# Attention maxima: which two of a unit's four PSUM banks share one maximum instruction

## Chip, core and metric

The kernel runs on one core of one Trainium2 chip. The metric is the device time of one execution in microseconds (us), the median of several runs. TensorE is called PE here, VectorE DVE, ScalarE ACT, GpSimd POOL, and SyncE, which issues most of the DMAs, SP.

## What is computed

One attention layer over 4096 tokens of 256 channels with 16 heads of 16, beside a mixture of experts, then a second layer with a convolution, a recurrence, an MLP and another mixture of experts. The change touches the first layer's attention alone:

```python
xd = (x @ W_down).reshape(b, t, h, s)
keys = jnp.einsum('bthk,hik->bthi', xd, tokeys) * scale
queries = jnp.einsum('bthk,hik->bthi', xd, toqueries) * scale
values = jnp.einsum('bthk,hik->bthi', xd, tovalues)
dot = jnp.einsum('bqhs,bkhs->bhqk', queries, keys)
attn = jax.nn.softmax(dot, axis=-1)
out = jnp.einsum('bhqk,bkhs->bqhs', attn, values).reshape(b, t, e)
return out @ W_unify + b_unify
```

The softmax subtracts each row's maximum. The kernel finds that maximum from a first computation of the scores and uses it in a second one.

## The kernel before

The whole program is a row of phases, of which `attention_phase` is by far the longest. It takes the 16 heads in 8 pairs and the 4096 queries in 8 chunks of 512; one pair and one chunk are a **round**, and there are 64 rounds. A round has `U` = 16 **units**. The two heads of a pair lie in rows 0 to 63 and 64 to 127 of the operands, so that matmuls of both can be in the array together.

In each unit run two streams of scores. The maximum stream is ahead of the other by `LEAD` = 24 units, and its first 24 units are done by the phase before this one, so that 1000 of this phase's 1024 units have it:

- The **maximum stream**: `max_part` (matmul L1120) computes for head h and key chunk j the scores of 128 queries by 512 keys into bank 2h + j of `SA`, a PSUM tile of four banks (`scores_q`). DVE reduces each bank to one maximum per query. These go to `MPART`, of which there are two buffers that take turns by round (`max_parts` and `attention_max_parts` in the profile).
- The **probability stream**: `score_tile` (matmul L1126) computes the transposed scores with the maximum already taken off, into one of three banks `ST` (`scores_t`), ACT takes the exponential (L1202, `probs`), and `pv_part` (L1136) multiplies by the values: eight matmuls per unit, four per key tile. The profile has two records for each of these, so that x8 there is one key tile and x16 are both.

All engines work in order. PE's order in a unit is: bank 0 of the maximum stream, a score tile, bank 1, a tile, bank 2, a tile, bank 3, a tile. Where the value matmuls stand is set by the parity of the unit's number (`u % 2`):

```python
BLOCKS = ({(0, 1): (0,), (1, 1): (1,)}, {(1, 0): (0, 1)})
```

A key is (head, key chunk), its value the key tiles whose four matmuls follow there. An even unit has one key tile behind bank 1 and one behind bank 3. An odd unit has both key tiles, eight matmuls, behind bank 2 and so ahead of bank 3.

PE may fill a bank when DVE has reduced it in the unit before: `max_part` waits for the count `sa_free`, and DVE waits for the count `sa_ready`, both four per unit and in the order of the banks. On DVE, `body` calls for each unit `reduce_first` (before: one instruction, L1235, over banks 0 and 1), then `reduce_rest` (before: L1242, twice, one for bank 2 and one for bank 3). Once per round, in the unit that begins a new one of the maximum stream (an even unit), `negative_max` (L1249) stands between the two calls; it reduces the parts of the whole round to the final negated maximum, which POOL splits and SP writes into the operands. Four times in 16 rounds, always at unit 12, `recip` (L1255) stands behind `reduce_rest`.

Of the kernel before, what the change touches and what calls it, by code (L numbers as in the profile page):

```python
# [10 lines left out]
ALU = mybir.AluOpType  # L11
ACT = mybir.ActivationFunctionType
AX = mybir.AxisListType
# [6 lines left out]
CH = 512  # L20
# [59 lines left out]
class Phase:  # L80
# [11 lines left out]
    def sb(self, name, shape, dt=F32):  # L92
        return self.stack.enter_context(self.nc.sbuf_tensor(f"{self.name}_{name}", shape, dt))
# [6 lines left out]
    def ps(self, name, shape=(P, CH), dt=F32):  # L100
        return self.stack.enter_context(self.nc.psum_tensor(f"{self.name}_{name}_sums", list(shape), dt))

    def sem(self, name):
        return self.stack.enter_context(self.nc.semaphore(f"{self.name}_{name}"))
# [824 lines left out]
def attention_phase(nc, q_scratch, k_scratch, v_scratch, max_scratch, den_scratch, recip_scratch, att_scratch, DISP, lead, outs,  # L929
# [10 lines left out]
    with Phase(nc, "attention") as ph:  # L940
# [6 lines left out]
        MPART = [sb("max_parts0", [P, 2, 4, 8]), lead.MPART]  # L947
# [6 lines left out]
        SA = ps("scores_q", [P, 4 * CH])  # L954
# [9 lines left out]
        sa_ready, sa_free = sem("scores_q_ready"), sem("scores_q_reduced")  # L964
# [20 lines left out]
        def halves(body):  # L985
            for i in range(NP // 2):
                body(i, i == NP // 2 - 1)
# [236 lines left out]
        @block.vector  # L1224
        def _(dve):
            nc.vector.memset(PR[:, 12:16, :], 1.0).then_inc(filled, 1)
            dve.sem_inc(sa_free, 4 * LEAD + 4)
            dve.sem_inc(neg_ready, 1)
            dve.sem_inc(pv_done, 3)
            dve.sem_inc(recip_out, 32)  # L1230

            def reduce_first(par, u, s):
                first = 2 * (u % 4)
                dve.wait_ge(sa_ready, 4 * s + 2)
                nc.vector.tensor_reduce(MPART[par][:, 0, u // 4, first:first + 2], SA[:, 0:2 * CH].rearrange("p (j k) -> p j k", j=2),  # L1235
                                        AX.X, ALU.max).then_inc(sa_free, 2)

            def reduce_rest(par, u, s):
                first = 2 * (u % 4)
                for j in range(2):  # L1240
                    dve.wait_ge(sa_ready, 4 * s + j + 3)
                    nc.vector.tensor_reduce(MPART[par][:, 1, u // 4, first + j:first + j + 1], SA[:, (2 + j) * CH:(3 + j) * CH],  # L1242
                                            AX.X, ALU.max).then_inc(sa_free, 1)

            def negative_max(par, s, splits):

                dve.wait_ge(sa_free, 4 * s + 8)
                dve.wait_ge(msplit, 2 * splits)
                nc.vector.tensor_reduce(NEG[:, :, :], MPART[par][:, :, :, :], AX.X, ALU.max, negate=True)\  # L1249
                    .then_inc(neg_ready, 1)  # L1250

            def recip(n):
                dve.wait_ge(den_in, 32 * (n + 1))
                dve.wait_ge(recip_out, 32 * (n + 1))
                nc.vector.reciprocal(RD[:, :], DEN[:, :]).then_inc(recip_done, 1)  # L1255

            def body(i, last):
                for r in range(HALF):
                    g = i * HALF + r
                    for u in range(U):  # L1260
                        s, s_round, s_unit = g * U + u + LEAD, r + (u + LEAD) // U, (u + LEAD) % U
                        has_max = not (last and s_round >= HALF)
                        if has_max:
                            reduce_first(s_round % 2, s_unit, s)
                        if s_unit == 0 and not (last and s_round > HALF):
                            negative_max((s_round - 1) % 2, s - 1, g + (u + LEAD) // U - 1)
                        if has_max:
                            reduce_rest(s_round % 2, s_unit, s)
                        if r % 4 == 1 and u == RECIP_AT:
                            recip(4 * i + r // 4)  # L1270

            halves(body)
# [1196 lines left out]
```

## Time and profile before

| | us |
|---|---|
| median of 3 runs | 3727.38 |
| lowest, highest | 3726.7, 3727.47 |
| profiled execution, its own time | 3727.63 |
| its span, first to last instruction | 3725.8 |
| PE busy | 3608.3 |
| DVE busy | 3209.2 |
| ACT busy | 2643.1 |
| mean granted clock of PE, share of full speed | 0.985 |

The page gives for each engine its busy time and, for each group of instructions, the idle time of the engine just before them with what ended it. Views of the trace give the same for a stretch, or the instructions one by one with their start. PEld is the loading of weights on PE, which may lie under a running matmul. The starts of matmuls are modelled from their records; an instruction's duration is longer than the distance to the next start where both overlap in the pipeline.

### The profile page before, as it was taken

How to read it: one execution, taken by the hardware profiler on the slowest of the kernel's cores; microseconds unless marked ns; L12 is line 12 of the kernel's file. 1: busy time of each engine (PE TensorE's matmuls, PEld its weight loads, DVE VectorE, ACT ScalarE, POOL GpSimd, SP SyncE). 2: the span in 40 equal slices, each digit the busy share in tenths (PEclk: the TensorE clock that was granted, in tenths of full speed). 3: DMA queues.
4: the chain of work that ended last, by engine and by line, in shares of the span. 5: the costliest groups of instructions: out<-in, count | busy, mean ns of one | idle time of the engine just before them, and what ended most of it. 6: DMA issues, size and time to landing. Idle time of an engine off the chain costs nothing. (4 is left out here: it accounts for less than half of the span.)

```text
span 3725.8 us, 78041 instructions
## 1 busy us (share of the span) xinstructions
PE 3608.3 (97%) x31366; PEld 2064.9 (55%) x31366; DVE 3209.2 (86%) x4509; ACT 2643.1 (71%) x4951; POOL 369.9 (10%) x331
## 2 busy tenths in 40 slices
PE   8799899999999999999999999999998989999998
PEld 6487444444444444444444444444445668888887
DVE  6667799999999999999999999999975757766664
ACT  3455598989888989888999888999896442223332
POOL 0123200000000000000000000000002203403323
PEclk9899899999999999999999999999999999999999
DMA  4910322021122113112202202200012000122332
GB/s 139 249 38 18 113 23 30 4 30 26 7 23 22 17 10 34 18 9 24 29 4 30 26 7 24 32 6 7 4 32 82 34 2 29 55 93 66 82 85 39
DMA packets 299888, 149.50 MB, mean 40 GB/s; under 512 B 218527, under 2 KB 278057, under 8 KB 296980
## 3 DMA queue, kind: packets, MB, share of 16 engines
q1 hardware_dynamic: 287252, 133.97, 19.4%
q0 software_dynamic: 12288, 10.70, 1.7%
q8 instruction: 240, 3.93, 0.5%
q14 instruction: 108, 0.88, 0.1%
HBM read 86.46 MB, written 64.18 MB: 40 GB/s over the span
## 5 line engine op out<-in xcount | busy, mean ns | idle before, releaser
L1202 ACT ACTIVATE probs<-attention_scores_t_sums 128x512 f32<-128x512 f32 x4096 | 2142.2, 597 | 246.0 <-PE attention_scores_t_sums L1126 243.8
L1126 PE MATMUL attention_scores_t_sums<-q_operand,k_operand 50*128 50x512 f32 x2048 | 702.9, 443 | 15.4 <-ACTq L1216 13.8
L1120 PE MATMUL attention_scores_q_sums<-attention_k_operand,attention_q_operand 48*128 48x512 f32 x2048 | 699.8, 439 | 0.0
L1126 PE MATMUL attention_scores_t_sums<-attention_q_operand,attention_k_operand 50*128 50x512 f32 x2048 | 698.6, 443 | 0.0
L1120 PE MATMUL attention_scores_q_sums<-k_operand,q_operand 48*128 48x512 f32 x1952 | 669.6, 440 | 0.0
L1242 DVE TENSOR_REDUCE max_parts<-attention_scores_q_sums 128x1 f32<-128x512 f32 x1008 | 639.1, 670 | 1.6 <-PE attention_scores_q_sums L1120 1.6
L1242 DVE TENSOR_REDUCE attention_max_parts<-attention_scores_q_sums 128x1 f32<-128x512 f32 x992 | 628.9, 670 | 0.0
L1235 DVE TENSOR_REDUCE max_parts<-attention_scores_q_sums 128x2 f32<-128x1024 f32 x504 | 605.7, 1202 | 8.6 <-PE attention_scores_q_sums L1120 8.5
L1136 PE MATMUL attention_o_psum_sums<-probs,attention_v_heads 128*32 128x256 f32 x8208 | 602.8, 388 | 0.0
L1136 PE MATMUL attention_o_psum_sums<-probs,v_heads 128*32 128x256 f32 x8192 | 602.1, 388 | 0.0
L1235 DVE TENSOR_REDUCE attention_max_parts<-attention_scores_q_sums 128x2 f32<-128x1024 f32 x496 | 596.8, 1203 | 0.0
L1120 PEld LDWEIGHTS attention_scores_q_sums<-attention_k_operand,attention_q_operand 48*128 48x128 f32 x2048 | 319.9, 184 | 388.8 <-issue 119.2
L1120 PEld LDWEIGHTS attention_scores_q_sums<-k_operand,q_operand 48*128 48x128 f32 x1952 | 306.3, 185 | 371.7 <-issue 115.7
L1126 PEld LDWEIGHTS attention_scores_t_sums<-q_operand,k_operand 50*128 50x128 f32 x2048 | 337.3, 185 | 17.3 <-ACTq L1216 14.0
L1126 PEld LDWEIGHTS attention_scores_t_sums<-attention_q_operand,attention_k_operand 50*128 50x128 f32 x2048 | 335.2, 184 | 19.7 <-ACT probs L1202 17.6
L1136 PEld LDWEIGHTS attention_o_psum_sums<-probs,v_heads 128*32 128x32 f32 x8192 | 187.6, 108 | 276.8 <-issue 148.7
L1136 PEld LDWEIGHTS attention_o_psum_sums<-probs,attention_v_heads 128*32 128x32 f32 x8208 | 188.1, 108 | 275.1 <-issue 147.7
L1096 POOL TENSOR_TENSOR attention_neg_max_split<-attention_neg_max,attention_zero 128x8 fp32r<-128x8 f32 x63 | 12.7, 202 | 2318.7 <-DVE attention_neg_max L1249 2318.7
L1975 ACT ACTIVATE mlp_silu<-mlp_gate_sums,mlp_b_gate 128x512 f32<-128x512 f32 x64 | 44.2, 691 | 200.1 <-PE mlp_gate_sums L119 200.1
L119 PE MATMUL experts_out_sums<-experts_w_low,experts_hidden_high 128*128 128x256 f32 x512 | 144.9, 283 | 0.0
L119 PE MATMUL experts_out_sums<-experts_w_high,experts_hidden_high 128*128 128x256 f32 x512 | 143.7, 281 | 0.0
L119 PE MATMUL experts_out_sums<-experts_w_high,experts_hidden_low 128*128 128x256 f32 x512 | 143.7, 281 | 0.0
(330 smaller groups left out, 4687.7 us busy)
## 6 DMA issues: line engine op xcount, KB each, us to landing
expert_rows<-attention_empty_rows SPq DMA_DIRECT2D x16, 516.0 KB, 5.6
v_scratch<-value_chunk SPq DMA_DIRECT2D x16, 512.0 KB, 5.4
w_whole<-in_L_ffn_ew SPq DMA_DIRECT2D x8, 1024.0 KB, 7.3
experts_w_whole<-in_L_ffn_ew SPq DMA_DIRECT2D x8, 1024.0 KB, 5.7
q_operand<-q_scratch SPq DMA_DIRECT2D x24, 256.0 KB, 4.7
k_operand<-k_scratch SPq DMA_DIRECT2D x24, 256.0 KB, 6.4
attention_q_operand<-q_scratch SPq DMA_DIRECT2D x24, 256.0 KB, 4.8
attention_k_operand<-k_scratch SPq DMA_DIRECT2D x24, 256.0 KB, 6.5
```

The costliest lines, as they stand in the source:

```text
L119: mm = nc.tensor.matmul(out, lhs[l], rhs[r], start=first and n == 0, stop=last and n == 2)
L1096: nc.gpsimd.tensor_tensor(MS[par][:, :, 0, :], NEG[:, :, :], ZERO[:, :, :], ALU.add).then_inc(msplit, 1)
L1120: nc.tensor.matmul(SA[:, (2 * h + j) * CH:(2 * h + j + 1) * CH], QOP[b][64 * h:64 * h + ROWS, qt * P:(qt + 1) * P], KOP[b][64 * h:64 * h + ...
L1126: nc.tensor.matmul(ST[bank_n][:, :], KOP[b][64 * h:64 * h + ROWS + 2, kt * P:(kt + 1) * P], QOP[b][64 * h:64 * h + ROWS + 2, c * CH:(c + 1 ...
L1136: mm = nc.tensor.matmul(OP[64 * h + 32 * side:64 * h + 32 * side + 32, :], VH[b][:, 2 * u + j, h, :], PR[:, u % 4 * 4 + 2 * (1 - h) + j, s ...
L1202: nc.scalar.activation(PR[:, tile, :], ST[bank_n][:, :], ACT.Exp).then_inc(st_free, 1)
L1235: nc.vector.tensor_reduce(MPART[par][:, 0, u // 4, first:first + 2], SA[:, 0:2 * CH].rearrange("p (j k) -> p j k", j=2), AX.X, ALU.max).th ...
L1242: nc.vector.tensor_reduce(MPART[par][:, 1, u // 4, first + j:first + j + 1], SA[:, (2 + j) * CH:(3 + j) * CH], AX.X, ALU.max).then_inc(sa_ ...
L1975: nc.scalar.activation(G[m % 2], GP[m % 2][:, :], ACT.Silu, bias=BG[:, m:m + 1])\
```

## The change

`reduce_first` now reduces bank 0 alone. `reduce_rest` reduces bank 1 alone, and then banks 2 and 3 with one instruction, which waits until both are full and releases both at once. The new helper `reduce_single` holds the instruction for banks 0 and 1. The four maxima of a unit go to the same places of `MPART` as before. The number of instructions, their shapes and the counts of the semaphores per unit stay as they are.

```diff
--- before.py
+++ after.py
@@ -1229,18 +1229,22 @@
             dve.sem_inc(pv_done, 3)
             dve.sem_inc(recip_out, 32)
 
+            def reduce_single(par, u, s, j):
+                part = 2 * (u % 4) + j
+                dve.wait_ge(sa_ready, 4 * s + j + 1)
+                nc.vector.tensor_reduce(MPART[par][:, 0, u // 4, part:part + 1], SA[:, j * CH:(j + 1) * CH],
+                                        AX.X, ALU.max).then_inc(sa_free, 1)
+
             def reduce_first(par, u, s):
+                reduce_single(par, u, s, 0)
+
+            def reduce_rest(par, u, s):
+                reduce_single(par, u, s, 1)
                 first = 2 * (u % 4)
-                dve.wait_ge(sa_ready, 4 * s + 2)
-                nc.vector.tensor_reduce(MPART[par][:, 0, u // 4, first:first + 2], SA[:, 0:2 * CH].rearrange("p (j k) -> p j k", j=2),
+                dve.wait_ge(sa_ready, 4 * s + 4)
+                nc.vector.tensor_reduce(MPART[par][:, 1, u // 4, first:first + 2],
+                                        SA[:, 2 * CH:4 * CH].rearrange("p (j k) -> p j k", j=2),
                                         AX.X, ALU.max).then_inc(sa_free, 2)
-
-            def reduce_rest(par, u, s):
-                first = 2 * (u % 4)
-                for j in range(2):
-                    dve.wait_ge(sa_ready, 4 * s + j + 3)
-                    nc.vector.tensor_reduce(MPART[par][:, 1, u // 4, first + j:first + j + 1], SA[:, (2 + j) * CH:(3 + j) * CH],
-                                            AX.X, ALU.max).then_inc(sa_free, 1)
 
             def negative_max(par, s, splits):
```

On DVE, the stretch of the attention in which a new round of the maximum stream begins (`attention_neg_max` is the final maximum, `max_parts` and `attention_max_parts` the two buffers of parts). Before:

```order
L1242 TENSOR_REDUCE attention_max_parts<-attention_scores_q_sums 128x1 [waits attention_scores_q_ready] x2
L1235 TENSOR_REDUCE max_parts<-attention_scores_q_sums 128x2 [waits attention_scores_q_ready]
L1249 TENSOR_REDUCE attention_neg_max<-attention_max_parts 128x8 [waits attention_neg_max_split_done,attention_scores_q_reduced]
L1242 TENSOR_REDUCE max_parts<-attention_scores_q_sums 128x1 [waits attention_scores_q_ready] x2
L1235 TENSOR_REDUCE max_parts<-attention_scores_q_sums 128x2 [waits attention_scores_q_ready]
```

After, at the same place:

```order
L1235 TENSOR_REDUCE attention_max_parts<-attention_scores_q_sums 128x1 [waits attention_scores_q_ready] x2
L1245 TENSOR_REDUCE attention_max_parts<-attention_scores_q_sums 128x2 [waits attention_scores_q_ready]
L1235 TENSOR_REDUCE max_parts<-attention_scores_q_sums 128x1 [waits attention_scores_q_ready]
L1253 TENSOR_REDUCE attention_neg_max<-attention_max_parts 128x8 [waits attention_neg_max_split_done,attention_scores_q_reduced]
L1235 TENSOR_REDUCE max_parts<-attention_scores_q_sums 128x1 [waits attention_scores_q_ready]
L1245 TENSOR_REDUCE max_parts<-attention_scores_q_sums 128x2 [waits attention_scores_q_ready]
```

The two-bank maximum has moved from the head of a unit to its end, and the final maximum now stands between the two single-bank ones.

On PE nothing moves. This is one odd unit, the same before and after: banks 0, 1 and 2 of `scores_q`, each with a tile of the other stream (`scores_t`), then the eight value matmuls, then bank 3 and its tile:

```order
L1120 MATMUL attention_scores_q_sums<-k_operand0,q_operand0 128x512 [waits attention_scores_q_reduced]
L1126 MATMUL attention_scores_t1_sums<-q_operand0,k_operand0 128x512 [waits attention_scores_t_used]
L1120 MATMUL attention_scores_q_sums<-k_operand0,q_operand0 128x512 [waits attention_scores_q_reduced]
L1126 MATMUL attention_scores_t2_sums<-q_operand0,k_operand0 128x512 [waits attention_scores_t_used]
L1120 MATMUL attention_scores_q_sums<-k_operand0,q_operand0 128x512 [waits attention_scores_q_reduced]
L1126 MATMUL attention_scores_t0_sums<-q_operand0,k_operand0 128x512 [waits attention_scores_t_used]
L1136 MATMUL attention_o_psum_sums<-probs,v_heads0 32x256 [waits attention_scores_t_used]
L1136 MATMUL attention_o_psum_sums<-probs,v_heads0 32x256 x7
L1120 MATMUL attention_scores_q_sums<-k_operand0,q_operand0 128x512 [waits attention_scores_q_reduced]
L1126 MATMUL attention_scores_t1_sums<-q_operand0,k_operand0 128x512 [waits attention_scores_t_used]
```

Each L1120 still waits for its own bank's count; what has changed is which maximum raises it.

## Rows read from the trace of the kernel before

**Rows 1.** Page, part 1: busy us, share, count by engine.
```profile
PE 3608.3 (97%) x31366; PEld 2064.9 (55%) x31366; DVE 3209.2 (86%) x4509; ACT 2643.1 (71%) x4951; POOL 369.9 (10%) x331
```

**Rows 2.** Stretch 1000 to 2500 us: engines' busy time (count), PEclk, DMA, GB/s.
```profile
1000.00:2500.00 1500.00, 1498.71 (x15376) 667.25 (x15376) 1498.00 (x1973) 1348.55 (x2603) 16.19 (x80) 1.00 0.19 20
```

**Rows 3.** Waits, 500 to 2760 us: total us, times, longest.
```profile
DVE max_parts L1235 <- PE attention_scores_q_sums L1120: 2.0, 6, 0.4
```

**Rows 4.** Timeline of DVE from 1504 us: start us, duration us, instructions.
```profile
1504.44 1.21 DVE L1235 TENSOR_REDUCE attention_max_parts<-attention_scores_q_sums 128x2 f32<-128x1024 f32 x1
1505.57 1.27 DVE L1242 TENSOR_REDUCE attention_max_parts<-attention_scores_q_sums 128x1 f32<-128x512 f32 x2
1506.77 1.21 DVE L1235 TENSOR_REDUCE attention_max_parts<-attention_scores_q_sums 128x2 f32<-128x1024 f32 x1
...
1509.10 1.21 DVE L1235 TENSOR_REDUCE attention_max_parts<-attention_scores_q_sums 128x2 f32<-128x1024 f32 x1
```

**Rows 5.** L1249 (one buffer), L1255: ns min/median/max, first and last start.
```profile
L1249 DVE TENSOR_REDUCE attention_neg_max<-max_parts x32: 194/197/220, 447.9 to 2768.8; 128x8 f32<-128x64 f32 x32
...
L1255 DVE RECIPROCAL recip_den<-denominators x16: 329/330/336, 495.9 to 2742.9; 128x32 f32<-128x32 f32 x16
```

**Rows 6.** Timeline of PE, 1505.8 to 1510 us: one odd and one even unit.
```profile
1505.84 0.49 PE L1120 MATMUL attention_scores_q_sums<-attention_k_operand,attention_q_operand 48*128 48x512 f32 x1
...
1506.17 0.40 PE L1120 MATMUL attention_scores_q_sums<-attention_k_operand,attention_q_operand 48*128 48x512 f32 x1
...
1506.41 0.40 PE L1120 MATMUL attention_scores_q_sums<-attention_k_operand,attention_q_operand 48*128 48x512 f32 x1
1506.74 1.07 PE L1136 MATMUL attention_o_psum_sums<-probs,attention_v_heads 128*32 128x256 f32 x16
1507.74 0.50 PE L1120 MATMUL attention_scores_q_sums<-attention_k_operand,attention_q_operand 48*128 48x512 f32 x1
...
1508.08 0.45 PE L1120 MATMUL attention_scores_q_sums<-attention_k_operand,attention_q_operand 48*128 48x512 f32 x1
...
1508.36 0.39 PE L1120 MATMUL attention_scores_q_sums<-attention_k_operand,attention_q_operand 48*128 48x512 f32 x1
...
1509.26 0.50 PE L1120 MATMUL attention_scores_q_sums<-attention_k_operand,attention_q_operand 48*128 48x512 f32 x1
...
1509.60 0.39 PE L1120 MATMUL attention_scores_q_sums<-attention_k_operand,attention_q_operand 48*128 48x512 f32 x1
```

**Rows 7.** Timeline of PEld, the load after 1507.98 us.
```profile
1508.03 0.18 PEld L1120 LDWEIGHTS attention_scores_q_sums<-attention_k_operand,attention_q_operand 48*128 48x128 f32 x1
```

**Rows 8.** Timeline of DVE, attention's start; in brackets idle time before.
```profile
426.37 1.29 DVE L1242 TENSOR_REDUCE max_parts<-attention_scores_q_sums 128x1 f32<-128x512 f32 x2 [0.43 <-PE attention_scores_q_sums L1120]
429.03 1.22 DVE L1235 TENSOR_REDUCE max_parts<-attention_scores_q_sums 128x2 f32<-128x1024 f32 x1 [1.38 <-PE attention_scores_q_sums L1120]
```

**Rows 9.** Timeline of PE, attention's start, granted clock 0.5.
```profile
423.38 0.79 PE L1120 MATMUL attention_scores_q_sums<-k_operand,q_operand 48*128 48x512 f32 x1
...
425.54 0.79 PE L1120 MATMUL attention_scores_q_sums<-k_operand,q_operand 48*128 48x512 f32 x1
...
428.29 0.62 PE L1120 MATMUL attention_scores_q_sums<-k_operand,q_operand 48*128 48x512 f32 x1
...
431.73 0.59 PE L1120 MATMUL attention_scores_q_sums<-k_operand,q_operand 48*128 48x512 f32 x1
```

**Rows 10.** L1235 into one of two buffers: count, durations, starts.
```profile
L1235 DVE TENSOR_REDUCE max_parts<-attention_scores_q_sums x504: 1148/1202/1225, 424.7 to 2766.3; 128x2 f32<-128x1024 f32 x168
```

**Rows 11.** Stretches behind the attention: busy one, one with a wait.
```profile
2893.00:2950.00 57.00, 53.89 (x271) 37.86 (x273) 56.65 (x11) 26.49 (x41) 16.93 (x4) 1.00 0.00 1
3046.00:3054.00 8.00, 5.88 (x21) 5.14 (x22) 6.89 (x6) 2.94 (x3) 0.00 (x0) 0.57 0.01 2
```

**Rows 12.** PE's waits, 2893 to 2950 us, then 3030 to 3060 us.
```profile
PE router_logit_parts_sums L1626 <- ACT router_hidden L1676: 3.1, 4, 0.8
...
PE mlp_squares_sums L1920 <- DVEq L2011: 3.9, 1, 3.9
```

## Prediction, made before the changed kernel ran

> **What bounds the kernel now.** I read the busy shares first: PE is busy for 97% of the span, DVE for 86%, ACT for 71% [rows 1]. These are means over stages that differ. In the attention, between 1000 and 2500 us, DVE is busy for 1498.00 of 1500 us, PE for 1498.71 and ACT for 1348.55, at a granted clock of 1.00 [rows 2]. PE and DVE both look full, so busy time alone doesn't name the bound. The waits do: from 500 to 2760 us DVE waits for PE for 2.0 us in all, in six places [rows 3]. DVE has its next maximum ready whenever it is done with the last one; it is the bound.
>
> The timeline of DVE shows its beat [rows 4]. A two-bank maximum (L1235) starts at 1504.44, 1506.77 and 1509.10 us, every 2.33 us, which is one unit. From its start to that of the first single-bank maximum (L1242) pass 1.13 us (1504.44 to 1505.57), and the two singles take the other 1.20 (1505.57 to 1506.77). An instruction's own time is a little longer, 1.21 us for two banks and 1.27 for two singles together, since its end lies under the start of the next. Two units, an odd and an even one, take 4.66 us. Over the whole stage, the final maxima of one buffer, one in every second round of 16 units, run 32 times from 447.9 to 2768.8 us [rows 5]; a round takes 2320.9 / 62 = 37.43 us, which is 8 pairs of units at 4.65 and 0.2 for the final maximum itself.
>
> Then PE's timeline of one pair [rows 6]. I call the four banks 0 to 3: 0 and 1 are the first head's, 2 and 3 the second's. In the odd unit L1120 fills bank 0 at 1505.84, bank 1 at 1506.17 and bank 2 at 1506.41; then come eight matmuls of probabilities with values (L1136, in the row as x16) at 1506.74, and only at 1507.74 is bank 3 filled. In the even unit banks 0 and 1 follow at 1508.08 and 1508.36, then four value matmuls, then banks 2 and 3 at 1509.26 and 1509.60. So **banks 0 and 1 are filled close together in both kinds of unit** (0.33 and 0.28 us apart), banks 2 and 3 in the even unit only (0.34 us); in the odd one they are 1507.74 - 1506.41 = 1.33 us apart. This decides the case, since a two-bank maximum needs both its banks full before it begins and gives both back only when it ends.
>
> **The change, part by part.**
>
> *Work of DVE.* Per unit one maximum over two banks and two over one bank, before and after, of the same shapes. Taken alone this is worth nothing: 1.13 + 1.20 = 2.33 us in either order.
>
> *The window of the pair.* Between the end of a two-bank maximum and the start of the next, both its banks must be filled again, if DVE isn't to stop. DVE gives 2.33 - 1.21 = **1.12 us** for that [rows 4]. Before, banks 0 and 1 need: 0.05 us from the end of the maximum (1506.77 + 1.21 = 1507.98) to PE's next weight load for L1120 (1508.03) [rows 4, 7]; 0.10 for loading weights into an idle array (a first matmul takes 0.49, a following one 0.39 [rows 6]); 0.33 or less to the second bank; 0.39 for its matmul; 0.12 until DVE starts (matmul at 428.29 for 0.62, so done at 428.91; L1235 at 429.03 [rows 8, 9]). Together at most 0.05 + 0.10 + 0.33 + 0.39 + 0.12 = 0.99 us. It fits in 1.12, which is why DVE hardly ever waits.
>
> After, banks 2 and 3 have to pass through the same window. In the **odd unit** the chain is: release 0.05; weights 0.10, and 0.33 from the matmul of bank 2 to the value matmuls (1506.41 to 1506.74); 1.00 from there to the matmul of bank 3 (1506.74 to 1507.74); 0.50 for that one [rows 6]; 0.12 to the start of the maximum. Sum 0.05 + 0.43 + 1.00 + 0.50 + 0.12 = 2.10 us. The window has 1.12, so **DVE stops for 0.98 us in every odd unit**. Nothing hides it: DVE works in order, and the next unit's bank 0 stands behind the waiting instruction, though it is full by then. PE can't make it up either; it can't fill bank 2 before the last maximum has read it.
>
> In the **even unit** the need is 0.05 + 0.10 + 0.24 + 0.39 + 0.12 = 0.90 us (0.24 being the closest spacing, 1506.17 to 1506.41 [rows 6]). It fits, with 0.22 to spare. PE is at bank 2 of the even unit in time: from bank 3 of the odd one it takes 1509.26 - 1507.74 = 1.52 us, and the maximum over the odd unit's banks ends 0.50 + 0.12 + 1.21 = 1.83 us after the same point.
>
> *Single maxima on banks 0 and 1.* Each bank has 2.33 - 0.67 = 1.66 us between its own maxima (a single takes 1.27 less the 0.60 by which the second starts later, 0.67 [rows 4]), and needs 0.05 + 0.50 + 0.12 = 0.67. That DVE may now begin after bank 0 alone, and that both banks come free earlier, gains nothing, as DVE isn't waiting there today [rows 3].
>
> *What moves with it.* The final maximum (L1249) now stands behind one single-bank maximum, not behind the pair; its 0.2 us per round stay in DVE's stream between an odd and an even unit and cost what they cost before, and POOL, which waits for it, has it a little sooner in the unit. The reciprocal (L1255, 0.33 us, 16 times [rows 5]) stands behind an even unit; its time will now lie in the stop of the odd unit that follows, a gain of 16 x 0.33 = 5 us. ACT has about 10% to spare [rows 2] and gets more.
>
> *The sum.* The code has one two-bank maximum per unit in 1024 - 24 = 1000 units, 504 of them in the one buffer [rows 10]; half of them are odd. 500 x 0.98 = 490, less 5, is **+485 us**. The profiled execution took 3727.63 us (span 3725.8), the median is 3727.38; so 3727.6 + 485 = about **4213 us**, 13.0% slower.
>
> *Bounds.* Three terms are not seen in just this position. The value matmuls after a lone matmul of bank 2 may start 0.24 instead of 0.33 us after it; DVE's start may take 0.04 (matmul at 425.54 for 0.79, done at 426.33; L1242 at 426.37 [rows 8, 9]) instead of 0.12: together 0.17 less, +400 us. The release may take 0.19 instead of 0.05 (1504.44 + 1.21 = 1505.65 to the matmul at 1505.84 [rows 4, 6], though PE was just leaving its value matmuls there): 0.14 more, +555 us. I take the middle values since they come from the same kind of instruction and wait: 0.12 is from a two-bank maximum, 0.05 from a release that PE stood ready for.
>
> **The rivals.**
>
> *No stop, 3722 to 3728 us.* DVE's work is the same, and the change only turns its pattern round against PE's. For it: DVE's floor of 4.66 us a pair is untouched, and the even unit fits in its window. It would decide if the matmul of bank 3 could come before the value matmuls in the odd unit. Against it: the order on PE is fixed in the code, and 2.10 us don't go into 1.12. This is also the case in which the kernel isn't slower. It ends within 0.2% of today's time, as only the 2.0 us of waits and the 5 us of reciprocals could go.
>
> *A smaller stop, 3970 to 4120 us.* If weights or matmul starts overlap the value block more than they do now, 0.2 to 0.5 us of the 0.98 vanish, each 0.1 us being worth 50 us. Nothing in the rows shows such an overlap: the x16 block is followed by L1120 after 1.00 us [rows 6].
>
> *The clock falls, over 4290 us.* PE will now idle twice in a pair, by about 0.3 us each: once before bank 2 of the even unit (1.83 + 0.05 against 1.52) and once before bank 2 of the odd one. At the lower clock level, 1.2 GHz, a pair took 431.73 - 423.38 = 8.35 us [rows 9], against 4.66 + 0.98 = 5.64. If a tenth of the pairs ran so, 50 x 2.7 = 135 us more, 4348 us; if half, 675 more. What speaks against it: from 2893 to 2950 us PE was busy for 53.89 of 57 us, with waits of up to 0.8 us, and the granted clock stayed at 1.00 [rows 11, 12]. It fell to 0.57 in the stretch from 3046 to 3054 us, where PE had waited 3.9 us at one piece [rows 11, 12]. The Trainium skill, TensorE: Matmul & The Clock Gate, section "A second HAM failure mode: psum-queue depth-cycling", says that a kernel which cycles through PSUM banks can idle so often in short pieces that the clock oscillates between its two levels. By that rule this change would pay twice, for the stop and for the clock; the stretch with 0.8 us waits at 1.00 disagrees with it for waits as short as these.
>
> *Even units stop too.* If their 0.22 us to spare are gone, each 0.1 us over costs 50 us. This lies in the upper part of the range.
>
> **How the numbers follow.** The stop in odd units (even units included if they add a little), 4120 to 4290: 0.87. Smaller stop: 0.04. Clock: 0.05. No stop: 0.04. The range 4110 to 4290 us takes in both bounds. A measurement of this kernel can tell about 0.2%, 7 us, from no change. Slower by more than that: 0.95; within it: 0.04; faster: 0.01, as nothing shortens DVE's stream by over 7 us.
>
> **What the profile after would show.** DVE's busy time stays near 3209 us, and its idle time before the two-bank maximum (now L1245), released by L1120, becomes about 490 us, in about 500 waits of nearly 1 us, none in even units. The two-bank maxima start alternately 2.33 and 3.31 us apart. The final maxima come every 8 x 5.64 + 0.2 = 45.3 us. The granted clock stays at 1.00. ACT's idle time before L1202 grows by nearly the whole 485 us. I am wrong if DVE waits in both kinds of unit (then PE is slower than its rows say), if the stop in the odd unit is far from 0.98, or if the clock leaves 1.00 during the attention.

## The result and the profile after

| | before | changed |
|---|---|---|
| median, us | 3727.43 (3726.7 to 3730.67, 4 runs) | 4213.09 (4210.83 to 4215.01, 4 runs) |
| profiled execution, us (span) | 3727.63 (3725.8) | 4215.01 (4213.2) |
| ratio, 95% interval | | 1.130, 1.1282 to 1.1318 |

The changed kernel is 485.7 us slower (4213.09 - 3727.43); 485 were forecast. These rows are from the page of the changed kernel: first busy time, share of the span and count by engine (compare [rows 1]), then groups of instructions: busy us, mean ns | idle time of the engine just before them and what ended it.

```profile
PE 3737.7 (89%) x31366; PEld 2027.9 (48%) x31366; DVE 3253.1 (77%) x4509; ACT 2701.5 (64%) x4951; POOL 369.3 (9%) x331
...
L1202 ACT ACTIVATE probs<-attention_scores_t_sums 128x512 f32<-128x512 f32 x4096 | 2200.7, 596 | 674.2 <-PE attention_scores_t_sums L1126 669.0
...
L1245 DVE TENSOR_REDUCE max_parts<-attention_scores_q_sums 128x2 f32<-128x1024 f32 x504 | 614.1, 1219 | 225.1 <-PE attention_scores_q_sums L1120 225.1
L1245 DVE TENSOR_REDUCE attention_max_parts<-attention_scores_q_sums 128x2 f32<-128x1024 f32 x496 | 604.2, 1218 | 222.4 <-PE attention_scores_q_sums L1120 222.4
...
L1235 DVE TENSOR_REDUCE max_parts<-attention_scores_q_sums 128x1 f32<-128x512 f32 x1008 | 645.1, 678 | 5.1 <-PE attention_scores_q_sums L1120 5.1
```

Nearly all the new idle time of DVE stands before the two-bank maximum, L1245: 225.1 + 222.4 = 447.5 us over the whole program. In the kernel before, the page has 8.6 us before its two-bank maximum, 2.0 of them between 500 and 2760 us [rows 3]. Before the single maxima there are 5.1 us. DVE's timeline shows where in the pair of units (compare [rows 4]):

```profile
1505.11 1.21 DVE L1245 TENSOR_REDUCE max_parts<-attention_scores_q_sums 128x2 f32<-128x1024 f32 x1
1506.24 1.28 DVE L1235 TENSOR_REDUCE max_parts<-attention_scores_q_sums 128x1 f32<-128x512 f32 x2
1508.40 1.22 DVE L1245 TENSOR_REDUCE max_parts<-attention_scores_q_sums 128x2 f32<-128x1024 f32 x1 [0.89 <-PE attention_scores_q_sums L1120]
1509.54 1.28 DVE L1235 TENSOR_REDUCE max_parts<-attention_scores_q_sums 128x1 f32<-128x512 f32 x2
1510.74 1.21 DVE L1245 TENSOR_REDUCE max_parts<-attention_scores_q_sums 128x2 f32<-128x1024 f32 x1
```

In the rows, DVE alternates between two-bank maxima (x1) and two single ones (x2), with one stop of 0.89 us. The two-bank maxima start 3.29 and 2.34 us apart in turn; a pair of units takes 1510.74 - 1505.11 = 5.63 us, before 4.66. PE's side of the stop, in the timelines of its matmuls and of its weight loads (compare [rows 6, 7]; the brackets give the idle time before and what ended it):

```profile
1504.05 0.49 PE L1120 MATMUL attention_scores_q_sums<-attention_k_operand,attention_q_operand 48*128 48x512 f32 x1 [0.34 <-DVE max_parts L1245]
...
1506.38 0.49 PE L1120 MATMUL attention_scores_q_sums<-attention_k_operand,attention_q_operand 48*128 48x512 f32 x1 [0.36 <-DVE max_parts L1245]
...
1506.80 1.07 PE L1136 MATMUL attention_o_psum_sums<-probs,v_heads 128*32 128x256 f32 x16
1507.80 0.50 PE L1120 MATMUL attention_scores_q_sums<-attention_k_operand,attention_q_operand 48*128 48x512 f32 x1
...
1506.37 0.18 PEld L1120 LDWEIGHTS attention_scores_q_sums<-attention_k_operand,attention_q_operand 48*128 48x128 f32 x1 [0.79 <-DVE max_parts L1245]
```

The first row is bank 2 of the even unit, the second that of the odd one. From there it is the chain of the prediction, link by link: the even unit's pair ends at 1505.11 + 1.21 = 1506.32; bank 2's weights load 0.05 us later; the value matmuls begin 0.43 us after that; bank 3 follows 1.00 us after them and takes 0.50, to 1508.30; DVE starts at 1508.40.

### The profile page after: what moved, and what is told of

Read it like the earlier page. It is cut to its first block and busy times, and to the rows that moved or that the text cites. A ratio compares the mean times of both kernels' runs of the same rounds, so it can differ in the third digit from the quotient of the medians.

```text
span 4213.2 us, 78041 instructions
## 1 busy us (share of the span) xinstructions
PE 3737.7 (89%) x31366; PEld 2027.9 (48%) x31366; DVE 3253.1 (77%) x4509; ACT 2701.5 (64%) x4951; POOL 369.3 (9%) x331
## 5 line engine op out<-in xcount | busy, mean ns | idle before, releaser
L1202 ACT ACTIVATE probs<-attention_scores_t_sums 128x512 f32<-128x512 f32 x4096 | 2200.7, 596 | 674.2 <-PE attention_scores_t_sums L1126 669.0
L1120 PE MATMUL attention_scores_q_sums<-attention_k_operand,attention_q_operand 48*128 48x512 f32 x2048 | 749.2, 444 | 183.9 <-DVE max_parts L1245 92.1
L1120 PE MATMUL attention_scores_q_sums<-k_operand,q_operand 48*128 48x512 f32 x1952 | 716.7, 446 | 172.9 <-DVE attention_max_parts L1245 86.4
L1245 DVE TENSOR_REDUCE max_parts<-attention_scores_q_sums 128x2 f32<-128x1024 f32 x504 | 614.1, 1219 | 225.1 <-PE attention_scores_q_sums L1120 225.1
L1245 DVE TENSOR_REDUCE attention_max_parts<-attention_scores_q_sums 128x2 f32<-128x1024 f32 x496 | 604.2, 1218 | 222.4 <-PE attention_scores_q_sums L1120 222.4
L1126 PE MATMUL attention_scores_t_sums<-q_operand,k_operand 50*128 50x512 f32 x2048 | 749.4, 446 | 15.6 <-ACTq L1216 13.8
L1126 PE MATMUL attention_scores_t_sums<-attention_q_operand,attention_k_operand 50*128 50x512 f32 x2048 | 743.5, 446 | 0.0
L1235 DVE TENSOR_REDUCE max_parts<-attention_scores_q_sums 128x1 f32<-128x512 f32 x1008 | 645.1, 678 | 5.1 <-PE attention_scores_q_sums L1120 5.1
L1235 DVE TENSOR_REDUCE attention_max_parts<-attention_scores_q_sums 128x1 f32<-128x512 f32 x992 | 635.8, 679 | 0.0
L1120 PEld LDWEIGHTS attention_scores_q_sums<-attention_k_operand,attention_q_operand 48*128 48x128 f32 x2048 | 322.4, 185 | 630.8 <-DVE max_parts L1245 209.3
L1120 PEld LDWEIGHTS attention_scores_q_sums<-k_operand,q_operand 48*128 48x128 f32 x1952 | 308.1, 185 | 598.8 <-DVE max_parts L1245 197.5
L1126 PEld LDWEIGHTS attention_scores_t_sums<-q_operand,k_operand 50*128 50x128 f32 x2048 | 321.3, 185 | 27.5 <-ACTq L1216 14.0
L1126 PEld LDWEIGHTS attention_scores_t_sums<-attention_q_operand,attention_k_operand 50*128 50x128 f32 x2048 | 320.1, 185 | 29.5 <-ACT probs L1202 17.5
```

The lines of the kernel that those rows point to most:

```text
L1120: nc.tensor.matmul(SA[:, (2 * h + j) * CH:(2 * h + j + 1) * CH], QOP[b][64 * h:64 * h + ROWS, qt * P:(qt + 1) * P], KOP[b][64 * h:64 * h + ...
L1126: nc.tensor.matmul(ST[bank_n][:, :], KOP[b][64 * h:64 * h + ROWS + 2, kt * P:(kt + 1) * P], QOP[b][64 * h:64 * h + ROWS + 2, c * CH:(c + 1 ...
L1202: nc.scalar.activation(PR[:, tile, :], ST[bank_n][:, :], ACT.Exp).then_inc(st_free, 1)
L1235: nc.vector.tensor_reduce(MPART[par][:, 0, u // 4, part:part + 1], SA[:, j * CH:(j + 1) * CH], AX.X, ALU.max).then_inc(sa_free, 1)
L1245: nc.vector.tensor_reduce(MPART[par][:, 1, u // 4, first:first + 2], SA[:, 2 * CH:4 * CH].rearrange("p (j k) -> p j k", j=2), AX.X, ALU.ma ...
```

## Experiments

All kernels were timed beside the kernel before, and their ratios are to it. What a **pair** of units took is worked out from the final maxima, which run every 16 units: (last start - first start) / 62 rounds, less 0.2 us, by 8; in b3 and b4, where DVE has time to spare for the final maximum, nothing is taken off. The 0.2 is the duration of the final maximum; by starts it costs DVE 0.12 to 0.13 us, which makes a pair 0.01 us longer throughout and changes no comparison.

| kernel | median, us | ratio, 95% interval | pair, us | expected, us |
|---|---|---|---|---|
| a1, new pair in even units only | 3915.40 | 1.0508 (1.0490 to 1.0525) | 5.03 | 3912 |
| a2, new pair in odd units only | 3914.05 | 1.0503 (1.0485 to 1.0520) | 5.03 | 3902 |
| b1, four singles | 3791.91 | 1.0176 (1.0159 to 1.0193) | 4.78 | 3797 |
| a3, singles, bank 2 late begun | 3945.29 | 1.0584 (1.0566 to 1.0601) | 5.09 | 3942 |
| a4, singles, bank 2 late released | 3981.43 | 1.0682 (1.0665 to 1.0700) | 5.16 | 3942 |
| b2, singles, both | 4245.23 | 1.1394 (1.1375 to 1.1413) | 5.69 | 4242 |
| b3, changed, value matmuls split | 3859.09 | 1.0357 (1.0339 to 1.0374) | 4.93 | 3862 |
| b4, before, value matmuls split | 3860.20 | 1.0356 (1.0339 to 1.0374) | 4.93 | 3862 |
| c1, changed, half of the block | 3997.35 | 1.0729 (1.0711 to 1.0747) | 5.20 | 3985 |
| c2, before, block behind bank 0 | 4339.66 | 1.1622 (1.1589 to 1.1655) | 5.80 | 4210 to 4270 |
| c3, changed, block behind bank 0 | 4122.04 | 1.1059 (1.1040 to 1.1077) | 5.39 | 4050 |

### Which unit pays (a1, a2)

The edit, shortened (the words in brackets stand for code):

```diff
 def reduce_first(par, u, s):
-    reduce_single(par, u, s, 0)
+    if u % 2 == 0: (bank 0 alone)            # a2: u % 2 == 1
+    else: (banks 0 and 1 together)
 def reduce_rest(par, u, s):
+    if u % 2 == 0: (bank 1, then banks 2 and 3 together)
+    else: (bank 2, bank 3)
```

> The changed pairing (banks 2 and 3 share a maximum) in even units only; odd units keep the pair over banks 0 and 1. Theory of the window: bank 2 comes free late, at the end of the even unit's pair, and in the odd unit that follows the eight value matmuls stand between banks 2 and 3. From the start of the even pair: 1.21 + 0.05 + 0.43 + 1.00 + 0.50 + 0.04 = 3.23 us until bank 3 of the odd unit can be reduced; DVE's own work until then is 1.13 + 1.13 + 0.60 = 2.86. A stop of 0.37 us in 500 pairs of units: +185 us, 3912 us. Rival 1 (only the late start counts, a pair waits for its second bank): the even unit fills banks 2 and 3 close together, so no cost, 3727 us. Rival 2 (a pair at the end of a unit costs by itself, whatever the unit): half of the 485 us, 3970 us.

> The changed pairing in odd units only. Theory of the window: bank 2 is released by the even unit's single maximum. From its start 0.67 + 0.05 + 0.43 + 1.00 + 0.50 + 0.10 = 2.75 us until both banks of the odd unit are full; DVE's own four singles take 2.40. A stop of 0.35 us in 500 pairs: +175 us, 3902 us. So the two halves of the change together cost less (360) than the whole (485). Rival 1 (only the late start counts): the whole cost, 4213 us. Rival 2 (each pair at the end of a unit costs the same): 3970 us.

Both rivals fall: neither kernel is at 3727 or 4213, nor at 3970. Each half costs 186 to 188 us, the whole 485: they don't add up. An estimate from the rows of the kernel before says why. There, from the start of the even unit's maximum over bank 2 to a full bank 3 in the odd unit, the chain over PE takes 0.67 + 0.05 + 0.43 + 1.00 + 0.50 + 0.04 = 2.69 us. DVE's own work in between is 0.60 + 0.60 + 1.13 + 0.60 = 2.93 us, so 0.24 are to spare. Each half moves the balance by about 0.60, one single maximum: a1 lengthens the chain, a2 takes work away from beside it. That leaves a stop of 0.60 - 0.24 = 0.36 us in each half, and 1.20 - 0.24 = 0.96 in the whole.

In a1 it is a *single* maximum that waits, bank 3's of the odd unit:

```profile
1505.90 2.43 DVE L1243 TENSOR_REDUCE attention_max_parts<-attention_scores_q_sums 128x2 f32<-128x1024 f32 x2
1508.25 0.68 DVE L1235 TENSOR_REDUCE attention_max_parts<-attention_scores_q_sums 128x1 f32<-128x512 f32 x1
1509.13 1.89 DVE L1235 TENSOR_REDUCE attention_max_parts<-attention_scores_q_sums 128x1 f32<-128x512 f32 x3 [0.21 <-PE attention_scores_q_sums L1120]
```

There the even unit fills its two banks close together and begins in time; what costs is that it gives bank 2 back late.

### What in the pair pays: its instruction, its late start, its late release (b1, a3, a4, b2)

Each unit has four single maxima, of the form below: one starts when `ready` banks of the unit are full, and raises `sa_free` by `freed`. Banks 0 and 1 have (1, 1) and (2, 1) in all four kernels. With (ready, freed) for bank 2 and bank 3: b1 (3, 1) and (4, 1); a3 (4, 1) and (4, 1); a4 (3, 0) and (4, 2); b2 (4, 0) and (4, 2).

```diff
+def reduce_single(par, u, s, h, j, ready, freed):
+    part = 2 * (u % 4) + j
+    dve.wait_ge(sa_ready, 4 * s + ready)
+    ins = nc.vector.tensor_reduce(MPART[par][:, h, u // 4, part:part + 1], SA[:, (2 * h + j) * CH:(2 * h + j + 1) * CH],
+                                  AX.X, ALU.max)
+    if freed:
+        ins.then_inc(sa_free, freed)
```

> Four single maxima, each with its own wait and its own release; no pair anywhere. Theory of the window: no stop, DVE alone sets the time with 8 x 0.60 = 4.80 us per pair of units against 4.66: +70 us, 3797 us. This is the base for the kernels with a late start or a late release. Rival (PE's or ACT's own limit was behind the cost): well above 3797.

> No two-bank maximum at all: four single ones, each releasing its own bank; but that of bank 2 waits until bank 3 is full as well, as the pair does. Theory of the window: DVE's own work is 8 x 0.60 = 4.80 us per pair of units (+70 us against 4.66); bank 2's maximum of the odd unit can start 0.67 + 0.05 + 0.43 + 1.00 + 0.50 + 0.04 = 2.69 us after that of the even unit, and DVE's own four singles take 2.40: a stop of 0.29. 5.09 us per pair, +215, 3942 us. Rival (the form: a two-bank instruction over banks 2 and 3 is what is slow): 3797 us, singles only.

> Four single maxima, each starting as soon as its own bank is full; but bank 2 is released only together with bank 3, as the pair does. Theory of the window: bank 3's maximum of the odd unit can start 0.67 + 0.05 + 0.43 + 1.00 + 0.50 + 0.04 = 2.69 us after that of the even unit, which released bank 2, against 2.40 of DVE's own work: a stop of 0.29. 5.09 us per pair, 3942 us, as with the late start. Rival 1 (only the late start counts): 3797 us. Rival 2 (the form of the instruction): 3797 us.

> Four single maxima, but bank 2's waits for bank 3 to be full and doesn't release: the late start and the late release of the pair, without its instruction. Theory of the window: from the start of bank 3's maximum in the even unit 0.67 + 0.05 + 0.43 + 1.00 + 0.50 + 0.04 = 2.69 us to the start of bank 2's in the odd one, DVE's own work 1.80: a stop of 0.89. 5.69 us per pair, +515, 4242 us; more than the sum of the two alone. Rival (the form of the instruction): 3797 us. Rival (the two parts add up): 70 + 145 + 145 = 360, 4087 us.

The form of the instruction is out: b2 has no two-bank maximum and still costs what the changed kernel does. Against b1, the late start costs 153 us, the late release 190, both together 453, more than their sum of 343. This is the same spare time again: with a single in place of the two-bank maximum DVE's work beside the chain is 5 x 0.60 = 3.00 us, not 2.93, which leaves 3.00 - 2.69 = 0.31 us to spare, so that each part alone stops DVE for 0.29 and both for 0.89.

The late release came 39 us above its number. What it had in place of the expected start of DVE is in these rows, first of a3, then of a4; in each the matmul of bank 3 and the maximum that waited for it:

```profile
1502.35 0.49 PE L1120 MATMUL attention_scores_q_sums<-attention_k_operand,attention_q_operand 48*128 48x512 f32 x1
...
1502.88 4.88 DVE L1235 TENSOR_REDUCE max_parts<-attention_scores_q_sums 128x1 f32<-128x512 f32 x8 [0.22 <-PE attention_scores_q_sums L1120]
```

```profile
1506.89 0.49 PE L1120 MATMUL attention_scores_q_sums<-attention_k_operand,attention_q_operand 48*128 48x512 f32 x1
...
1507.49 0.69 DVE L1235 TENSOR_REDUCE max_parts<-attention_scores_q_sums 128x1 f32<-128x512 f32 x1 [0.29 <-PE attention_scores_q_sums L1120]
```

From the end of the matmul to the start are 0.04 us in a3 (1502.84 to 1502.88) and 0.11 in a4 (1507.38 to 1507.49), for the same shape. The maximum of a4 raises its count by 2, that of a3 by 1. In b2, the maximum that waits raises nothing, and it starts 0.04 after its matmul too (1504.85 + 0.50 = 1505.35 to 1505.39). The two-bank maximum of the changed kernel raises by 2 and has 0.10 (1508.30 to 1508.40). I had put 0.04 for a4; 500 x 0.07 = 35 us are most of the difference. One more thing differs between a3 and a4 at this place: the maximum ahead of the waiting one raises its count in a3 and not in a4. This was not tested alone.

### Where the value matmuls stand (b3, b4)

```diff
-BLOCKS = ({(0, 1): (0,), (1, 1): (1,)}, {(1, 0): (0, 1)})
+BLOCKS = ({(0, 1): (0,), (1, 1): (1,)}, {(0, 1): (0,), (1, 1): (1,)})
```

b3 has this on the changed kernel, b4 on the kernel before.

> The changed kernel, but the odd unit's value matmuls stand as the even unit's do, four behind bank 1 and four behind bank 3, so that nothing stands between banks 2 and 3. Theory of the window: banks 2 and 3 need 0.90 to 0.99 us in a window of 1.12, no stop of this kind; but PE now changes between scores and values four times per pair of units, not three, so PE sets the time: 2 x (0.24 x 2 + 0.33 x 2 + (0.57 + 0.10) x 2) = about 4.93 us. +135 us, 3862 us. Rival (the pairing over banks 2 and 3 costs wherever the value matmuls stand): 4213 us or more.

> The kernel before with the same placement of the value matmuls, four behind bank 1 and four behind bank 3 in both kinds of unit. Theory of the window: PE's four changes set the time here too, 4.93 us per pair of units, 3862 us: with this placement the two pairings cost the same, within 10 us. Rival (the pairing as such): 3727 to 3862, and the changed kernel with this placement some 485 us above it.

With nothing between banks 2 and 3, the new pairing costs nothing against the old: 3859.09 and 3860.20 us. Both are some 134 us slower than the kernel before, since PE changes four times per pair between the two kinds of matmul, not three, and now sets the time. (The terms of the expectation for b3 add up to 4.96 us, not to 4.93; the rows of b3 give 4 x (0.34 + 0.32 + 0.57) = 4.92.) As PE sets the time, a stop of DVE below 4.93 - 4.66 = 0.27 us per pair would not show in the total; the 0.98 of the changed kernel would. The trace settles the rest: from 500 to 2700 us, DVE waited before L1245 four times, for 1.8 us in all. Stretch 500 to 2700 us of b3: busy time of PE, PEld, DVE, ACT and POOL, then granted clock, DMA share, GB/s.

```profile
500.00:2700.00 2200.00, 2199.66 (x21398) 813.24 (x21398) 2159.82 (x2745) 1947.84 (x3623) 22.33 (x110) 1.00 0.18 19
```

PE is busy throughout there, and DVE has 2200 - 2160 = 40 us to spare.

### How long the block is (c1)

In the odd unit, only one of the two key tiles is multiplied, so four of the eight value matmuls are missing and the attention's sums lack that tile. (The flag that starts the sums was moved to the tile that is left; this part of the edit is not shown.)

```diff
-BLOCKS = ({(0, 1): (0,), (1, 1): (1,)}, {(1, 0): (0, 1)})
+BLOCKS = ({(0, 1): (0,), (1, 1): (1,)}, {(1, 0): (1,)})
```

> The changed kernel with half of the odd units' value matmuls left out (one key tile's four of the eight between banks 2 and 3; the sums lack that tile). Theory of the window: the chain gets 0.43 us shorter (0.57 from the value matmuls to bank 3, not 1.00): a stop of 0.55, 5.18 us per pair of units, +265 less 5, 3985 us. So 0.43 us less between the banks takes away 0.43 us per pair in full, 215 to 225 us. Rival (PE's total work sets the time): PE was never full in the changed kernel, and no change, 4213 us.

```profile
1501.91 1.28 DVE L1235 TENSOR_REDUCE max_parts<-attention_scores_q_sums 128x1 f32<-128x512 f32 x2
1503.65 1.22 DVE L1245 TENSOR_REDUCE max_parts<-attention_scores_q_sums 128x2 f32<-128x1024 f32 x1 [0.46 <-PE attention_scores_q_sums L1120]
```

The wait fell from 0.89 to 0.46 us, by exactly the 0.43 by which the block is shorter, and the time by 216 us = 500 x 0.43. The 3985 us expected were a slip in the sum: 500 x 0.55 less 5 is 270, and 3727 + 270 = 3997, which is what was measured.

### The same trap for the old pairing (c2, c3)

```diff
-BLOCKS = ({(0, 1): (0,), (1, 1): (1,)}, {(1, 0): (0, 1)})
+BLOCKS = ({(0, 1): (0,), (1, 1): (1,)}, {(0, 0): (0, 1)})
```

c2 has this on the kernel before, c3 on the changed one.

> The kernel before (pair over banks 0 and 1), but with the odd unit's eight value matmuls behind bank 0, so that they now stand between the banks of that pair. Theory of the window: 0.05 + 0.43 + 1.00 + 0.50 + 0.10 = 2.08 us in a window of 1.12, a stop of 0.96 or a little more, since PE comes to bank 0 of the odd unit straight from four value matmuls and may be 0.1 us late: 5.63 to 5.75 us per pair, 4210 to 4270 us. The old pairing then costs what the new one does. Rival (the pairing at the unit's end is what costs): 3727 us.

> The changed kernel with the same placement, the odd unit's eight value matmuls behind bank 0. The pair over banks 2 and 3 now has its banks close together in both kinds of unit; the value matmuls stand between banks 0 and 1, which have single maxima. Theory of the window: no stop before the pair beyond 0.05 us. But by PE's order four and eight value matmuls now stand close to each other around bank 0, and bank 1 of the odd unit comes late for its single maximum: a stop of about 0.6 there, 5.3 us per pair, 4050 us; below the old pairing with the same placement by 100 to 220 us. Rival (the pairing at the unit's end is what costs): 4213 us and more.

The direction is as expected: with the block behind bank 0, the old pairing is the slower one, by 218 us, and the two-bank maximum over banks 0 and 1 stops as the new one does in the changed kernel:

```profile
1502.46 1.22 DVE L1235 TENSOR_REDUCE attention_max_parts<-attention_scores_q_sums 128x2 f32<-128x1024 f32 x1 [1.03 <-PE attention_scores_q_sums L1120]
...
1508.55 1.23 DVE L1235 TENSOR_REDUCE attention_max_parts<-attention_scores_q_sums 128x2 f32<-128x1024 f32 x1 [1.34 <-PE attention_scores_q_sums L1120]
```

Both sizes were missed, c2 by 70 us beyond its upper end and c3 by 72. For c2 the trace accounts for nearly all of it:

- The usual pair takes 5.78 us, not at most 5.75 (at 2655.26 and 2661.04 us two such stops end). PE comes to bank 0 of the odd unit 0.15 us late from its value matmuls, not 0.1 (it was free at 1504.80 + 1.21 + 0.05 = 1506.06 and its matmul starts at 1506.21). That is about 15 us.
- One odd unit per round waits longer, here 1.34 for 1.03 us, together about 20 us. It is unit 1, where the value matmuls also wait for ACT's copy of the last round's sums (`o_copied`): PE waited for that copy 46 times between 500 and 2700 us, and never in the kernel before.
- The clock fell once in the attention, to 0.50 from 2669.8 to 2683.5 us. Two stops there were 3.53 and 3.27 us long, about 5 us more than usual in all.
- What follows the last final maximum, the last units without maxima among it, ran at a low clock for longer: 4341.1 - 3349.6 = 991 us to the end, where the kernel before has 957 and the changed one 955. That is 34 us. The row shows its first part; the last three figures are the granted clock, the share of the DMA engines and GB/s:

```profile
3345.00:3410.00 65.00, 62.10 (x359) 22.12 (x355) 3.71 (x6) 37.95 (x73) 9.79 (x6) 0.63 0.15 36
```

Three of c2's four executions, the profiled one among them, took 4337 to 4343 us at a mean clock of 0.976 to 0.978; the fourth took 4316.49 at 0.985. That it lacked the low stretch is likely, but it has no profile.

In c3 the end is longer too, 4121.9 - 3133.9 = 988 us, 31 more than before, at 0.50 from 3155 to 3180 us. Most of the rest is the pair, 5.39 us for 5.3: 0.62 are the stop before bank 1, as put, 0.06 a short delay of the two-bank maximum behind the even unit's singles (1504.56 to 1505.82 are 1.26, not 1.20), and unit 1 has its longer wait here as well (0.85 for 0.53).

## Why the prediction was right

**The bound.** That DVE was the engine to look at, and that only the start of the two-bank maximum counted, held: 447.5 us of its new idle time stand before L1245.

**The window.** The time that refilling banks 2 and 3 needs in the odd unit was put at 0.05 + 0.43 + 1.00 + 0.50 + 0.12 = 2.10 us; the rows of the changed kernel give 0.05 + 0.43 + 1.00 + 0.50 + 0.10 = 2.08. The stop by starts was put at 0.98 and is 0.97 (after 1506.24 two singles take 0.60 each, to 1507.44, and 1508.40 is 0.96 later; over the pair 5.63 - 4.66 = 0.97). c1 and b3 show that the block between the banks is the cause, and a3, a4 and b2 that it works by late start and late release together.

**The even unit.** It fits with its 0.22 us to spare: of 1000 two-bank maxima 504 waited, all 500 of the odd units and four of even ones (the first of the attention for 1.37 us, three others for 0.26 each). Two places in which PE idles were named; they are there, with 0.34 and 0.36 us.

**The middle values of the uncertain terms.** The release (0.05) and the distance from bank 2 to the value matmuls (0.33 beside 0.10 of weights) were right as taken, and so was the start of DVE, for a reason not known then: 0.11 belongs to an instruction that raises a count by 2, 0.04 to one that raises it by 1. The lower bound of that term didn't apply. That the reason is the raise by 2 rests on a3, a4 and b2, with the reservation made there.

**Final maxima** were to come every 45.3 us; they start from 452.7 to 3257.8 us, which is 45.2.

**How close, and how much of it is luck.** 485 forecast and 485.7 measured are closer than the terms are known: a term read to 0.01 us is worth 5 us over 500 units, and the four executions lie 4 us apart. Two terms were a little off, in opposite directions: the stop was 0.97 for 0.98 (5 us too much), and the 16 reciprocals gave back 3 us and not 5, since a stop behind one shows as 0.69 us in place of 0.89 (16 x 0.20). The mechanism and its size are no luck; the match to 1 us is.

**What was off.** The idle time before L1245 was to be about 490 us and is 447.5: the view counts from the end of the instruction before, which lies 0.08 us behind the next possible start, so a stop of 0.97 shows as 0.89. The page's idle time understates such a stop. DVE's busy time was to stay near 3209 us and is 3253.1, for the same reason: 500 x 0.08 = 40 us that lay under another instruction now stand alone. ACT's idle time before L1202 grew by 674.2 - 246.0 = 428 us, not by nearly 485; the busy time of L1202 grew by 2200.7 - 2142.2 = 58 us at the same mean of one (596 and 597 ns), so fewer of them overlap. And the granted clock did leave 1.00, once, in the attention behind its first 25 us (at the attention's start it is low in both kernels). By the prediction's own words this is a sign of being wrong; it was worth about 1 us:

```profile
1715.00:1721.00 6.00, 4.98 (x50) 2.00 (x48) 5.10 (x8) 4.65 (x9) 0.41 (x2) 1.00 0.02 1
1721.00:1725.50 4.50, 4.33 (x32) 1.81 (x32) 2.48 (x5) 2.47 (x6) 0.00 (x0) 0.62 0.28 1
1725.50:1732.00 6.50, 5.80 (x60) 2.40 (x60) 5.62 (x9) 4.85 (x10) 0.00 (x0) 1.00 0.18 14
```

DVE's next stop was 2.02 us long and not 0.89:

```profile
1724.33 1.22 DVE L1245 TENSOR_REDUCE attention_max_parts<-attention_scores_q_sums 128x2 f32<-128x1024 f32 x1 [2.02 <-PE attention_scores_q_sums L1120]
```

Before it PE had had waits of at most 0.5 us. So the argument from waits of 0.8 us at 1.00 [rows 11, 12] was too strong: such waits don't exclude a fall. The Trainium skill (TensorE: Matmul & The Clock Gate, "A second HAM failure mode: psum-queue depth-cycling") says that a kernel which cycles through PSUM banks can idle so often in short pieces that its clock oscillates. This trace shows one fall of at most 4.5 us in some 2800 us, and no oscillation.

None of the kernels tried here is faster than the one before.

## What to carry to other kernels

An instruction that covers two buffers needs both full before it starts and holds both until it ends; what the producer must do between the two buffers has to fit into the consumer's time for everything else. So compare, in the producer's order, the distance between the two fills with that window, before asking what the instructions cost. Two halves of a change can cost more together than one by one (186 and 188 us here, 485 together), because each alone first uses up time to spare that the other needs too.

## What the runs showed of the hardware

- A waiting VectorE instruction that raises a semaphore by 2 started 0.11 us after the matmul that it waited for had ended (a4), one that raises it by 1 after 0.04 us (a3), one that raises none after 0.04 (b2), all of the same shape, 128x512 to 128x1. a4 and b2, in which a single maximum raises by 2, have 79041 instructions in the profile, a3 and b1 78041: one more for each of the 1000 such maxima. That this instruction takes the 0.07 us is likely and not shown.
- In the attention, behind its first 25 us, the granted clock fell in 4 of the 13 profiled kernels: once in the changed one (between 1721 and 1725.5 us), twice in b2, once in c2 (for 13.7 us) and three times in c3. All four have short waits of PE. In c3 each fall came about 2 us after a wait of 0.99 us for ACT (PE resumed at 1119.12, 1812.19 and 2505.28 us), in the changed kernel right behind one of 0.49, and in b2, the first time, right behind one of 0.55 (PE resumed at 685.01 us). But c1 has the same waits as the changed kernel (0.34 and 0.36 us in a pair, 0.5 at most) and no fall, so such waits alone don't decide it. What does stays open.
- In c2 the clock stayed at 0.50, its lower level of 1.2 GHz, from 3360 to 3400 us, while PE was busy for 38.96 of these 40 us by the profile. A busy PE alone didn't bring the clock back there; this wasn't followed up.
